# A fused decoder layer: keys and values inside a state recurrence as three products of split parts, one buffer for the states, and five smaller moves

## What is computed

```python
x = x + mamba(layernorm(x))              # d_inner 1024, 16 states, causal conv of 4
#   h[t] = h[t-1] * exp(A * dt[t]) + (x[t] * dt[t]) * B[t];  y[t] = sum_n h[t][n] * C[t][n]
k = ctx @ Wk + bk ; v = ctx @ Wv + bv    # ctx 8 x 750 x 256 -> 512, 16 heads of 32
x = x + softmax(q(layernorm(x)) @ k.T / sqrt(32)) @ v @ Wo + bo
g = softmax(gelu(z @ rW1 + rb1) @ rW2 + rb2)   # z = layernorm(x): router, best 2 of 4
x = x + sum over chosen e of g_e * (gelu(z @ We1[e] + be1[e]) @ We2[e] + be2[e])
```

## Time and profile before

| | |
|---|---|
| median of 3 runs (lowest, highest) | 2679.37 us (2675.36, 2680.34) |
| the profiled execution | 2675.31 us, its span 2673.5 us |
| TensorE clock granted, mean over the span | 0.948 of full |
| busy share: PE, PE weight loads, DVE, ACT, POOL | 90%, 74%, 54%, 46%, 51% |
| recurrence: first scan starts, last scan ends | 324.0 us, 998.8 us |
| attention: first instruction | 1017.2 us |
| experts: first instruction | 1826.1 us |

### The profile page before, as it was taken

How to read it: one execution, slowest core, us unless ns; L and a number is a source line. 1 busy time by engine, 2 the same in 40 slices (tenths; PEclk the granted TensorE clock), 3 DMA queues, 4 the chain that set the end, 5 groups by cost and what they waited for, 6 DMA issues and landing times. The chain is left out here.

```text
span 2673.5 us, 39214 instructions
## 1 busy us (share of the span) xinstructions
PE 2404.6 (90%) x14240; PEld 1976.3 (74%) x14240; DVE 1452.0 (54%) x2034; ACT 1219.3 (46%) x2645; POOL 1373.0 (51%) x947
## 2 busy tenths in 40 slices
PE   7999499999999997589999999884989989998994
PEld 6867388888888885457766667564878878888883
DVE  7714599999999982355766666644121121121222
ACT  4345377777777651334544444433323333333331
POOL 2323477777777773365556656635460450019712
PEclk9999699999999998689999999886989999999997
DMA  4326956666666563455554655605230130003413
GB/s 121 125 69 220 268 177 208 195 188 174 200 199 207 165 188 101 129 116 122 136 135 115 143 120 124 156 21 170 79 112 22 63 118 16 16 31 95 116 34 118
DMA packets 235990, 341.72 MB, mean 128 GB/s; under 512 B 34706, under 2 KB 164306, under 8 KB 234690
## 3 DMA queue, kind: packets, MB, share of 16 engines
q1 hardware_dynamic: 213250, 279.89, 37.6%
q0 software_dynamic: 13728, 47.19, 5.7%
q10 hardware_dynamic: 8864, 12.72, 1.4%
HBM read 212.08 MB, written 127.65 MB: 127 GB/s over the span
## 5 line engine op out<-in xcount | busy, mean ns | idle before, releaser
L917 DVE TENSOR_TENSOR_SCAN s_h<-s_decay,s_ub 128x928 f32<-128x928 f32 x256 | 527.3, 2080 | 13.9 <-PE s_ub L944 7.1
L955 PE MATMUL s_yps<-s_hc,identity 128*128 128x224 f32 x2016 | 423.1, 353 | 0.0
L2080 DVE TENSOR_TENSOR e_hl<-e_ps,e_hh 128x256 fp32r<-128x256 f32 x256 | 108.6, 425 | 571.6 <-ACT e_ps L2130 571.2
L847 ACT ACTIVATE s_decay<-s_dt,s_A 128x224 f32<-128x224 f32 x1024 | 387.9, 470 | 20.8 <-DVE s_h L917 18.8
L955 PEld LDWEIGHTS s_yps<-s_hc,identity 128*128 128x128 f32 x2016 | 362.5, 190 | 0.8 <-issue 0.5
L1299 DVE TENSOR_REDUCE t_nmax<-t_ps 112x1 fp32r<-112x752 f32 x256 | 240.3, 938 | 218.8 <-PE t_ps L1633 218.0
L1255 POOL TENSOR_TENSOR t_part<-t_pT 125x672 f32<-125x672 f32 x128 | 206.9, 1616 | 275.1 <-ACT t_pT L1543 271.7
L2129 ACT ACTIVATE e_hh<-e_ps,e_b 128x256 fp32r<-128x256 f32 x256 | 122.0, 477 | 432.7 <-PE e_ps L2156 432.4
L2154 PE MATMUL e_ps<-e_xTh,e_w1h 128*128 128x256 f32 x1024 | 292.9, 286 | 23.3 <-DVE e_xTl L2072 23.3
L1543 ACT ACTIVATE t_pT<-t_ps 125x448 f32<-125x448 f32 x384 | 181.2, 546 | 273.7 <-PE t_ps L1659 266.9
L804 POOL TENSOR_TENSOR s_hc<-s_h,s_Cc 128x896 f32<-128x896 f32 x128 | 247.5, 1939 | 90.2 <-DVE s_h L917 47.4
(11 more groups left out here) (231 smaller groups left out, 4607.3 us busy)
## 6 DMA issues: line engine op xcount, KB each, us to landing
s_ut<-ut_d SPq DMA_DIRECT2D x192, 128.0 KB, 3.3
carry<-in_L_ffn_We POOLq DMA_DIRECT2D x24, 1024.0 KB, 5.7
t_k<-kh_d SPq DMA_DIRECT2D x64, 375.0 KB, 6.3
xs_d<-s_zero SPq DMA_DIRECT2D x30, 512.0 KB, 3.6
ut_d<-a_x SPq DMA_DIRECT2D x32, 448.0 KB, 5.4
kh_d<-s_kh SPq DMA_DIRECT2D x32, 375.0 KB, 2.8
kl_d<-s_kl SPq DMA_DIRECT2D x32, 375.0 KB, 3.1
v_d<-s_v SPq DMA_DIRECT2D x48, 250.0 KB
```

Of the source, the lines that this page charges most:

```text
L847: ins = nc.scalar.activation(decay[:, u % 2, :, n, 2:SLOT], dts[:, u % 2].rearrange("p (s t) -> p s t", s=NSEG), ACT.Exp, scale=A[:, u % C ...
L917: nc.vector.tensor_tensor_scan(h[:, u % 2, k].rearrange("p n t -> p (n t)"), decay[:, u % 2, k].rearrange("p n t -> p (n t)"), ub[:, s % 2 ...
L955: ins = nc.tensor.matmul(yps[:, u % 2, 0:L], ident[:], hc[:, u % 2, :, n], start=(n == 0), stop=(n == NS - 1))
```

## The change

1. **Keys and values as three products.** The weights and the context are split once into a high part (float32r, rounded by ACT) and a low part (the rest, float32r, by POOL), and each product is high x high + low x high + high x low. PE's `keys_values` takes one such product ("third") per segment k = 1, 2, 3, in unit 0 all three at k = 3. Keys are computed on 376 + 376 columns, where there were 375 + 375, with two zero columns. Six copies or subtractions at the stage's start are new, and for each further batch one copy on ACT (`high_context`, in the first unit but one, ahead of its decays) and one subtraction on POOL (`low_context`, ahead of the batch's first product).
2. **One place for the states.** `h` has one place for each segment. A scan now waits for POOL's product of the same segment one unit earlier, where the first scan of a unit waited for all products of two units earlier. The raw context has one place as well, its next load waits for the split.
3. **Last sums in halves**: 2 x 16 matmuls of 112 columns instead of 4 x 16 of 56.
4. `load_next_stage` is issued one unit later each.
5. **Second rows** of the attention: x of batch 1 is loaded at sl = 9 of the prelude, ahead of values and weights.
6. The two extra rows of `k3` are written by ACT (4 activations of 2 x 1500 elements, ahead of the scaling of Wq), not by POOL.
7. The `gelu` of the last batch but one stands at sl = 4 in iteration 8, not at sl = 0.
8. **Bias**: DVE's wait for `b2` stands ahead of each tile's results, not behind the gates.

```diff
-        h = sb("h", [P, 2, NSEG, NS, SLOT])
+        h = sb("h", [P, NSEG, NS, SLOT])
...
+            def low_weights(i):
+                high, low, w = ((wkh, wkl, wk_raw), (wvh, wvl, wv_raw))[i]
+                pool.wait_ge(w_high, i + 1)
+                nc.gpsimd.tensor_tensor(low[:], w, high[:].bitcast(F32), ALU.subtract).then_inc(w_split, 1)
+
+            def low_context(b):
+                pool.wait_ge(ctx_high, b + 1)
+                if b >= 1:
+                    pool.wait_ge(v_mm, NC * b)
+                nc.gpsimd.tensor_tensor(cxl[:, :, 0:CTX], cxT, cxh[:, :, 0:CTX].bitcast(F32), ALU.subtract).then_inc(ctx_split, 1)
+
+            low_weights(0)
+            low_context(0)
+            low_weights(1)
             for u in range(UNITS):
                 b = u // CC
+                if u % CC == 0 and b >= 1:
+                    low_context(b)
...
+            def high_context(b):
+                act.wait_ge(ctx_loaded, 16 * (b + 1))
+                if b >= 1:
+                    act.wait_ge(v_mm, NC * b)
+                    act.wait_ge(ctx_split, b)
+                nc.scalar.activation(cxh[:, :, 0:CTX], cxT, ACT.Copy).then_inc(ctx_high, 1)
...
                 if u >= 2:
                     keys_values(u - 2)
+                if u % CC == 1 and u > 1 and u < UNITS:
+                    high_context(u // CC)
                 if u < UNITS:
                     decays(u)
+                    if u == 0:
+                        high_weights()
+                        high_context(0)
...
-                if u >= 2:
-                    dve.wait_ge(hc_done, NSEG * (u - 1))
                 for k in range(NSEG):
                     s = NSEG * u + k
                     dve.wait_ge(fill_done, s + 1)
+                    if u >= 1:
+                        dve.wait_ge(hc_done, s - NSEG + 1)
...
-                for k in range(NSEG):
-                    pe.wait_ge(hc_done, NSEG * u + k + 1)
-                    if k == 0:
-                        pe.wait_ge(y_done, u - 1)
+                pe.wait_ge(y_done, u - 1)
+                for half in range(2):
+                    pe.wait_ge(hc_done, NSEG * u + 2 * half + 2)
...
+                    w, cx = ((wkh, cxh), (wkl, cxh), (wkh, cxl))[third]
+                    for a in range(2):
+                        for k in range(CK):
+                            ins = nc.tensor.matmul(kvps[:, a, 0:EVEN], w[:, k, q * P:(q + 1) * P], cx[:, k, a * EVEN:(a + 1) * EVEN],
+                                                   start=(third == 0 and k == 0), stop=(third == 2 and k == CK - 1))
...
+                if it == -1 and sl == 9:
+                    load_x(1)
...
-                if sl == 14 and among(a + 1, B):
+                if sl == 14 and it >= 0 and among(a + 1, B):
                     load_x(a + 1)
...
-                if sl == 0 and among(last, B):
+                if sl == (4 if it == B else 0) and among(last, B):
                     gelu(last)
```

More of the change, by code:

```diff
@@ L766, in _ @@
                     store_keys_values(u - 1)
-                if b == B - 1 and 1 <= c <= 5:
-                    load_next_stage(c - 1)
+                if b == B - 1 and 2 <= c <= 6:
+                    load_next_stage(c - 2)
                 if u % 2 == 1 and u // 2 < ZEROS:
@@ L976, in keys_values @@
                 if u % 2 == 0:
-                    if pieces[0] == 0 and u >= 1:
+                    if third == 0 and u >= 1:
                         pe.wait_ge(v_done, NC * b + V_TILES[q][0])
-                    for i in pieces:
-                        a, k = i // 2, i % 2
-                        ins = nc.tensor.matmul(kvps[:, a, 0:HALF], wk[:, k, q * P:(q + 1) * P],
-                                               cxT[b % 2][:, k, a * HALF:(a + 1) * HALF], start=(k == 0), stop=(k == CK - 1))
@@ L984, in keys_values @@
+                    if third == 2:
                         ins.then_inc(k_mm, 1)
                 else:
[L986 removed]
+                    if third == 0:
                         pe.wait_ge(k_split, KC * b + q + 1)
[L988 to L994 removed]
+                    cx, w = ((cxh, wvh), (cxh, wvl), (cxl, wvh))[third]
@@ L996, in _ @@
+                    for t in V_TILES[q]:
+                        for k in range(CK):
+                            ins = nc.tensor.matmul(kvps[0:CT, t % 2], cx[:, k, t * CT:(t + 1) * CT], w[:, k],
+                                                   start=(third == 0 and k == 0), stop=(third == 2 and k == CK - 1))
+                        if third == 2:
+                            ins.then_inc(v_mm, 1)
             fill(0)
@@ L1003, in _ @@
                         sums(u - 1, range(4 * k - 4, 4 * k))
-                    if k >= 1:
-                        keys_values(u, (range(0, 1), range(1, 2), range(2, 4))[k - 1])
+                    if k >= 1 and u >= 1:
+                        keys_values(u, k - 1)
+                    if k == 3 and u == 0:
+                        for third in range(3):
+                            keys_values(u, third)
                     if NSEG * u + k + 2 < NSEG * UNITS:
@@ L1582, in probabilities @@
                 nc.scalar.activation(p[:], p[:], ACT.Exp).then_inc(exped, 1)
+            two = slice(ROWS3, ROWS3 + 2)
+            for r in range(4):
+                nc.scalar.activation(k3[two, :, r], ident[two, 0:2].unsqueeze(2).to_broadcast([2, 2, CTX]), ACT.Identity, scale=0.0,
+                                     bias=ident[two, ROWS3 + r % 2:ROWS3 + r % 2 + 1]).then_inc(rows_set, 1)
             act.wait_ge(w_loaded, 16 * N_W)
```

94 lines of the change are left out of this document (43 added, 51 removed).

## The result

| | before | changed |
|---|---|---|
| median of 4 runs (lowest, highest) | 2679.86 us (2675.36, 2681.37) | 2643.23 us (2636.87, 2646.16) |
| ratio, 95% interval | | 0.9863 (0.9841 to 0.9885) |
| profiled execution, span | 2675.31, 2673.5 us | 2644.08, 2642.3 us |

A forecast was written before the change was run, and what follows sets the result against it. PE was taken to bound the recurrence, with DVE close behind. The terms summed to -42.3 us on the profiled 2675.3, or 2633.0; with the median's offset the forecast was 2636 us, range 2618 to 2658.

The forecast's parts named there:

- Keys and values, -21.6: Recurrence: cheaper matmuls save PE 3.8 us a batch, DVE then sets the pace, 2.7 us gained in each of 8.
- The one place for `h`: Recurrence: scans waiting for the same segment's product one unit earlier cost nothing, as long as POOL isn't late.
- Start, +6.5: First batch: three POOL subtractions of 8.0 us delay products, a scan by 3.4 us and PE's keys; 6.5 us lost.
- Later batch starts, +3: Later batches: a POOL subtraction of 3.4 us ahead of the first product costs .4 us each, 7 times.
- Last sums, -7.2: End of recurrence: 64 records of twice the columns cost .112 us each as before, gaining 7.2 us.
- Second rows, -20: Attention: earlier x removes most of DVE's 23.65 us wait, 3 to 4 us stay for the third group's keys.
- Gelu, -3: Attention, iteration 8: moved off ACT's path ahead of a row PE waits 3.56 us for, gaining 3 us.
- `k3`'s rows, 0: Attention's prelude: writing the rows on ACT instead of POOL costs nothing, scaling of Wq still ends early enough.
- `b2` and `load_next_stage`, 0: Experts' bias wait and later stage loads: no cost, b2 lands before the gates end, the loads have a unit to spare.
- the wait only changes its name: Rival, attention: third group's keys or values stop PE instead, 10 of the 20 us come back; 2646 us, chance .18.
- more than the wait: Rival, attention: the low clock behind x's wait goes too, up to 8 us more gained; 2628 us, chance .14.

The follow-up runs named there:

- r1: Changed kernel with keys and values made by float32 matmuls again; a batch takes 85.24 us, against 82.17 in the changed kernel.
- r2: Changed kernel without the product of the weights' low part, 28 fewer PE matmuls a batch; a batch takes 82.06 us.
- r5: Changed kernel with both weights' low parts subtracted by DVE before its first scan, not by POOL; first batch 82.67 us against 90.05, whole kernel 2642.05 us.
- r3: Changed kernel with x of batch 1 loaded late again, behind values and weights; attention 801.0 us against 790.0.
- r4: Changed kernel with POOL's addition of the bias to x moved behind the row sum; attention 777.3 us against 790.0, whole kernel 2628.30 us.
- r9: Changed kernel with x of batch 1 loaded late and POOL's bias addition behind the row sum; attention 798.6 us.
- r8: Changed kernel with seven loads of later steps' weights moved behind the keys of the third group; attention 779.7 us against 790.0.
- r7: Changed kernel with last sums in quarters, k3's rows on POOL and the gelu's old place; last scan to attention 18.2 us, attention 793.2 us.
- r11: Changed kernel with one more, already met, DVE wait ahead of each scan; a batch takes 82.19 us against 82.17.

## Why the prediction held, point by point

- **Keys and values, -21.6.** Right in kind: DVE took over from PE, and r1 and r2 show both sides. DVE's chain was taken as 81.6 us from the waits and came out as 82.05 to 82.17, so a batch gives 2.2 us and not 2.7. Of this .4 us are the slightly longer units, whose cause is open. The one place for `h` cost nothing, as said: DVE has no wait for POOL between 408 and 990 us.
- **Start, +6.5.** The steps came as written: three subtractions of 7.9 us (8.0), a wait of 3.08 us (3.4), PE's keys behind the last of them. The first batch takes 7.9 us more than a later one, and 7.4 of them go with two subtractions (r5; 4.6 to 7.5 against all kernels with the three). What was missing is that late products hold PE's sums, and these the fills: 3.17 us more for DVE.
- **Later batch starts, +3.** Wrong, they cost nothing: the first two units of every later batch take 9.92 and 10.59 us like the others, and PE's weight loads wait for POOL there 1.8 us in seven batches; its matmuls have no such wait in the list.
- **Last sums, -7.2.** Right: -7.4, and .114 us a record of 112 columns where one of 56 took .112, so the columns don't set it. The rule of the Trainium skill ("TensorE: Matmul & The Clock Gate", section "LDWEIGHTS (loading the stationary operand)") that I weighed gave the same gain, and the trace agrees with it, .112 and .114 us beside its 107 ns.
- **Second rows, -20.** Right in kind and near in size, 17.4 and 18.5 us by step 24 in two pairs (the changed kernel against r3, r4 against r9), with the new wait where it was put, the keys of the third group, 4.5 us for 3 to 4 (r8). Over the whole stage the pairs differ by 11.0 and 21.3, which one run each can't tell from scatter. What the sum lacks is a step: I added the attention's edits as if its later steps kept their durations. They lost 6.8 to 9.2 us between steps 24 and 88 in all six kernels with this attention. Outputs held by POOL added 8.1 us of busy time on DVE in the changed kernel, and with POOL's addition moved the loss there is 1.4 and 1.6 us (r9, r4).
- **Gelu, -3.** Too much. Its wait of 3.56 us is gone, PE waits 3.0 us for POOL's sums instead, and .7 us are left (r7).
- **`k3`'s rows, 0.** Wrong: 2 to 3 us by the hold, 3.3 at step 0 between the two kernels and 5.1 in r7, with the clock in it. I looked at who waits for these rows, and not at who runs beside POOL while it makes them.
- **`b2` and `load_next_stage`, 0**: not told from nothing; the experts' 1.3 us lie in their scatter (847.0 to 848.9 in the kernels that don't touch their gates).

Of the rivals, "the wait only changes its name" was a fifth true (4.5 of 23 us), and "more than the wait" was true up to step 5 (28.6 us for a wait of 23.65), behind which nothing of it was left. Of the 11 us by which the sum missed the profiled execution, 2.6 lie in the recurrence, 4.4 in the attention, and 4.3 in the first stretch and the experts, which the change hardly touches. That the attention came within 4.4 is luck in part: what the early load gave beyond its wait and the 3.3 us at step 0 had not been counted, and the new gap, the held outputs and the gelu took more than that.

## What to carry to other kernels

When an engine is relieved, the gain ends at the chain of the next engine, and that chain is its period less its waits; check it by relieving the first engine a second time. Read the cost of a short series from its neighbours' starts, not from its own span, for its first record can lie over what stands ahead of it. An instruction that lasts ten times as long as its siblings may be held, as the ones here were, and costs like a wait, though no list of waits shows it: compare the longest with the usual duration in each group, and look at what the neighbour engine does in that time. Compare a stretch first in all kernels that leave it alone: here that was 8 us of an attention, and pieces of the stage told more than the whole. Before moving an edit's gain into a sum, ask which pairs of instructions lie within a microsecond of each other further on.

## What the hardware showed

Some DVE instructions whose operands lie in SBUF are held while POOL works through tensor instructions, and end when one of POOL's has ended: an addition of 128x224 takes .34 us alone and up to 3.67 beside POOL, a comparison of 112x64 elements .22 and 5.14, one of 112x2 elements .17 at rest in the changed kernel, .46 where the end of an addition of POOL met it, and 3.46 in r7_small. DVE instructions that read PSUM, such as the scans and the low keys of the recurrence, ran beside POOL's products at their usual 2.09 and 1.00 us. Operands in SBUF alone don't make a held instruction: the norm's statistics of 112x512 elements (L1354) read SBUF, began beside a tensor instruction of POOL in 20 of 32 places of the changed kernel, and took .68 or .69 us there as in the other twelve. The Trainium skill's "GPSIMD Engine Reference", section "1. Specifications", says that GpSimd shares its SBUF interfaces with VectorE and names contention with DVE instructions "in a 2-port perf mode or with two SBUF inputs"; the comparison has two SBUF inputs, and the trace agrees. Whether the two others run in such a mode no row here shows.

A wait that is already met costs DVE nothing that shows: 256 more of them changed a batch by .02 us (r11).
